# The batch loop of a normalise, project and gate kernel, written out

## What is computed

```
g = group_norm(x, 32 groups, eps=1e-5)            # over 4 channels and all pixels of a batch
u, var = mean and variance of g over the channels, for each pixel (ddof=1)
n = (g - u) / (sqrt(var) + 1e-6)
out = x + g * (einsum('bchw,oc->bohw', n, W) + b)
```

## Time and profile before

| | |
|---|---|
| median of three runs | 2007.43 us (2003.10 to 2016.56) |
| the profiled execution | 2013.78 us |
| its span, first to last instruction | 2012.0 us |
| mean granted TensorE clock | 0.977 |
| VectorE busy | 1774.8 us, 88% |
| TensorE busy | 1762.1 us, 88% |
| GpSimd busy | 1456.2 us, 72% |
| ScalarE busy | 1433.4 us, 71% |
| read / written | 398.80 MB / 268.44 MB, 332 GB/s over the span |

### The profile page before, as it was taken

One profiled execution on the slowest core, in us unless ns is written; L12 is line 12 of the kernel. 1 busy time (PEld: TensorE's weight loads), 2 busy tenths in 40 slices (PEclk: granted clock), 3 DMA queues, 4 the chain that ended last, 5 costly groups with the idle time before them and its releaser, 6 DMA issues.

```text
span 2012.0 us, 61495 instructions
## 1 busy us (share of the span) xinstructions
PE 1762.1 (88%) x22562; PEld 998.3 (50%) x22562; DVE 1774.8 (88%) x2120; ACT 1433.4 (71%) x2498; POOL 1456.2 (72%) x1684
## 2 busy tenths in 40 slices
PE   0089998999789997999979999699998999899997
PEld 0055555555445554555535555355554555455553
DVE  5669989999879997899869998799987999898896
ACT  5598876888568884788838887488875888544441
POOL 0068777888668876688758887588876888688885
PEclk9989999999999998999989999899998999999999
DMA  9989998999879998899978999699997999844665
GB/s 379 372 323 354 375 349 290 412 374 385 326 266 395 372 391 288 310 386 376 379 260 328 385 390 355 240 381 376 382 343 253 409 353 393 315 190 189 263 248 203
DMA packets 184241, 671.78 MB, mean 334 GB/s; under 512 B 20688, under 2 KB 21072, under 8 KB 183888
## 3 DMA queue, kind: packets, MB, share of 16 engines
q1 hardware_dynamic: 110160, 398.85, 53.7%
q10 hardware_dynamic: 73728, 268.47, 33.7%
HBM read 398.80 MB, written 268.44 MB: 332 GB/s over the span
## 4 chain that ended last, share of the span: by engine, by line
PE 48%; DVE 20%; issue 12%; DMA 11%; POOL 3%; ACT 3%; SPq 2%; ACTq 1%; POOLq 0%; DVEq 0%
PE proj_ps L753 27%; PE sums_ps L742 12%; PE factor_ps L728 8%; DMA tiles<-x 7%; DVE scaled L652 7%; DMA out<-tiles 4%; DVE bn L696 4%; DVE tiles L665 3%; DVE bn L697 3%; SPq L428 2%; ACT unused L529 1%; POOL tiles L472 1%; POOL tiles L461 1%; ACT squares L544 1%; DVE gn L600 1%
## 5 line engine op out<-in xcount | busy, mean ns | idle before, releaser
L753 PE MATMUL proj_ps<-scaled,w_t 128*128 128x512 f32 x2048 | 1014.6, 619 | 0.2 <-DVE scaled L652 0.2
L472 POOL TENSOR_SCALAR tiles<-tiles,out_shift 128x1024 f32<-128x1024 f32 x512 | 576.8, 1127 | 242.3 <-DVE tiles L665 232.5
L665 DVE SCALAR_TENSOR_TENSOR tiles<-proj_ps,gate_shift,tiles 128x1024 f32<-128x1024 f32 x512 | 643.8, 1257 | 50.4 <-PE proj_ps L753 48.3
L544 ACT ACTIVATE squares<-tiles 128x1024 f32<-128x1024 f32 x512 | 537.3, 1049 | 195.3 <-POOL tiles L461 77.5
L461 POOL TENSOR_SCALAR tiles<-tiles,norm_scalars 128x1024 f32<-128x1024 f32 x512 | 614.6, 1201 | 81.5 <-DMA tiles<-x 67.6
L652 DVE TENSOR_TENSOR scaled<-tiles,factor_ps 128x1024 f32<-128x1024 f32 x512 | 619.8, 1211 | 58.2 <-PE factor_ps L728 41.3
L529 ACT ACTIVATE unused<-tiles,bn 128x1024 uint8<-128x1024 f32 x560 | 634.8, 1134 | 0.6 <-DVE bn L697 0.6
L753 PEld LDWEIGHTS proj_ps<-scaled,w_t 128*128 128x128 f32 x2048 | 356.8, 195 | 253.2 <-issue 252.2
L728 PE MATMUL factor_ps<-pieces,pick_sb 128*128 128x128 bf16 x4096 | 323.2, 223 | 138.6 <-DVE scaled L652 72.5
L742 PEld LDWEIGHTS sums_ps<-tiles,const_sb 128*32 128x32 f32 x8192 | 196.2, 110 | 404.9 <-issue 274.6
L728 PEld LDWEIGHTS factor_ps<-pieces,pick_sb 128*128 128x128 bf16 x4096 | 234.8, 99 | 250.3 <-issue 128.6
(11 more groups left out here) (56 smaller groups left out, 693.2 us busy)
## 6 DMA issues: line engine op xcount, KB each, us to landing
tiles<-x SPq DMA_DIRECT2D x760, 512.0 KB, 9.4
out<-tiles ACTq DMA_DIRECT2D x512, 512.0 KB, 7.0
const_sb<-const SPq DMA_DIRECT2D x1, 193.5 KB, 2.3
scaled<-w SPq DMA_DIRECT2D x1, 64.0 KB, 2.2
scaled<-ident SPq DMA_DIRECT2D x1, 64.0 KB, 2.0
pick_sb<-pick SPq DMA_DIRECT2D x1, 8.0 KB, 2.1
bias_sb<-bias SPq DMA_DIRECT2D x1, 0.5 KB, 2.1
```

Source lines behind the costliest of these rows:

```text
L472: nc.gpsimd.tensor_scalar(place(s), place(s), 1.0, out_shift[:, 0:1], ALU.mult, ALU.add).then_inc(finished, 1)
L544: nc.scalar.activation(squares[:, step % 2, :], place(step), ACT.Square).then_inc(squared, 1)
L665: nc.vector.scalar_tensor_tensor(out=place(s), in0=proj_ps[:, s % 2, :], scalar=gate_shift[:, 0:1], in1=place(s), op0=ALU.add, op1=ALU.mul ...
L753: mm = nc.tensor.matmul(proj_ps[:, s % 2, h:h + BANK], w_t[:, :], scaled[:, s % 2, h:h + BANK], start=True, stop=True)
```

## The change

The loop is gone. `over_periods` calls `period` for every batch from -1 to 8 with a plain number, so each engine's instructions for batches 1 to 6 stand in the program one after the other. Each wait value and address is a constant. `wait_apart` is replaced by the plain wait everywhere, and the semaphore `wait_passed`, which nobody waited for, is dropped. Which operations are issued, their order on each engine and what each waits for stay.

```diff
-        wait_passed = sem("wait_passed")
...
-        def wait_apart(eng, semaphore, value):
-
-
-            eng.wait_ge(semaphore, value)
-            if not isinstance(value, int):
-                eng.sem_inc(wait_passed, 1)
...
-        def over_periods(eng, period, looks_ahead=False):
-
-
-
-            looped = batches - 1 - looks_ahead
-            ahead = {"more": True} if looks_ahead else {}
-            no_more = {"more": False} if looks_ahead else {}
-            period(-1, own=False, before=False, nxt=True, **(ahead if batches > 1 else no_more))
-            period(0, own=True, before=False, nxt=batches > 1, **(ahead if batches > 2 else no_more))
-            if looped > 1:
-                with eng.Fori(1, looped) as b:
-                    period(b, own=True, before=True, nxt=True, **ahead)
-            for b in range(max(looped, 1), batches):
-                period(b, own=True, before=True, nxt=b < batches - 1, **no_more)
-            period(batches, own=False, before=True, nxt=False, **no_more)
+        def over_periods(period, looks_ahead=False):
+
+            for b in range(-1, batches + 1):
+                ahead = {"more": b + 2 < batches} if looks_ahead else {}
+                period(b, own=0 <= b < batches, before=b > 0, nxt=b + 1 < batches, **ahead)
...
         def at_batch(array, b, s):
-            if isinstance(b, int):
-                return array[b, :, columns(s)]
-            return array[bass.ds(b, 1), :, columns(s)].rearrange("a c n -> (a c) n")
+            return array[b, :, columns(s)]
...
-                wait_apart(pool, gated, b * slots + step - LAG_OUT + 1)
+                pool.wait_ge(gated, b * slots + step - LAG_OUT + 1)
```

More of the change, by code:

```diff
@@ L204, in bn_before @@
     def bn_before(n):
-        return 0 if isinstance(n, int) and n == 0 else n * plan.bn_slots + (first_plan.bn_slots - plan.bn_slots)
+        return 0 if n == 0 else n * plan.bn_slots + (first_plan.bn_slots - plan.bn_slots)
     def act_before(n):
-        if isinstance(n, int) and n == 0:
+        if n == 0:
             return 0
@@ L397, in wait_item_done @@
             def wait_item_done(n, i):
-                of = first_plan if isinstance(n, int) and n == 0 else plan
+                of = first_plan if n == 0 else plan
                 if of.engine[i] == "dve":
-                    wait_apart(sp, bn_done, bn_before(n) + (of.index[i] + 1))
+                    sp.wait_ge(bn_done, bn_before(n) + (of.index[i] + 1))
                 else:
-                    wait_apart(sp, act_done, act_before(n) + 2 * (of.index[i] + 1))
+                    sp.wait_ge(act_done, act_before(n) + 2 * (of.index[i] + 1))
             def wait_buffer_free(tenant, b):
                 for (kind, i), back in places.predecessors(tenant):
-                    if not isinstance(b, int) or 0 <= b - back + (kind == "stats") < batches:
+                    if 0 <= b - back + (kind == "stats") < batches:
                         break
@@ L417, in wait_buffer_free @@
                     n = b - back if kind == "stream" else b - back + 1
-                    wait_apart(sp, stored[p], (n * len(stores[p]) + stores[p].index(s) + 1) * 16)
+                    sp.wait_ge(stored[p], (n * len(stores[p]) + stores[p].index(s) + 1) * 16)
             def load(tenant, b):
@@ L440, in period @@
                         load(tenant, b + 1)
-            over_periods(sp, period, looks_ahead=True)
+            over_periods(period, looks_ahead=True)
             for p in range(BUFFERS):
@@ L450, in norm @@
                 if s == 0:
-                    wait_apart(pool, gn_step, (batch + 1) * GN_STEPS)
+                    pool.wait_ge(gn_step, (batch + 1) * GN_STEPS)
                     if own:
-                        wait_apart(pool, normed, batch * slots)
+                        pool.wait_ge(normed, batch * slots)
                     nc.gpsimd.tensor_copy(norm_scalars[:, :], new_scalars[:, 0:2]).then_inc(norm_scalars_set, 1)
-                    wait_apart(pool, norm_scalars_set, batch + 1)
+                    pool.wait_ge(norm_scalars_set, batch + 1)
                 if s in streamed_slots:
                     turn, uses = places.turn(("stream", s), "stream")
-                    wait_apart(pool, stream_loaded[held_by(s)], (batch * uses + turn + 1) * 16)
+                    pool.wait_ge(stream_loaded[held_by(s)], (batch * uses + turn + 1) * 16)
                 nc.gpsimd.tensor_scalar(place(s), place(s), norm_scalars[:, 0:1], norm_scalars[:, 1:2],
@@ L466, in finish @@
                     if before:
-                        wait_apart(pool, finished, b * slots)
+                        pool.wait_ge(finished, b * slots)
                     nc.gpsimd.tensor_copy(out_shift[:, :], mean).then_inc(out_shift_set, 1)
-                    wait_apart(pool, out_shift_set, b + 1)
-                wait_apart(pool, gated, b * slots + step - LAG_OUT + 1)
+                    pool.wait_ge(out_shift_set, b + 1)
+                pool.wait_ge(gated, b * slots + step - LAG_OUT + 1)
                 nc.gpsimd.tensor_scalar(place(s), place(s), 1.0, out_shift[:, 0:1],
@@ L475, in correct @@
             def correct(done):
-                wait_apart(pool, approx_done, done)
-                wait_apart(pool, miss_done, done)
+                pool.wait_ge(approx_done, done)
+                pool.wait_ge(miss_done, done)
                 nc.gpsimd.tensor_tensor(miss[:, :], miss[:, :], approx[:, :], ALU.mult).then_inc(miss_scaled, 1)
-                wait_apart(pool, miss_scaled, done)
+                pool.wait_ge(miss_scaled, done)
                 nc.gpsimd.tensor_tensor(miss[:, :], miss[:, :], approx[:, :], ALU.mult).then_inc(miss_squared, 1)
             def split_first(done):
-                wait_apart(pool, piece_a_done, done)
+                pool.wait_ge(piece_a_done, done)
                 nc.gpsimd.tensor_tensor(factor[:, :], factor[:, :], piece[:, :], ALU.subtract).then_inc(rest_done, 1)
             def split_second(done, step):
-                wait_apart(pool, piece_b_done, done)
+                pool.wait_ge(piece_b_done, done)
                 nc.gpsimd.tensor_tensor(pieces[:, (step - LAG_FIT) // SPLIT % 2, :], factor[:, :], piece[:, :],
@@ L502, in period @@
                     if root_of is not None:
-                        wait_apart(pool, root_sq_done, root_of)
+                        pool.wait_ge(root_sq_done, root_of)
                         nc.gpsimd.tensor_tensor(miss[:, :], var[:, :], miss[:, :], ALU.subtract).then_inc(miss_done, 1)
@@ L510, in period @@
                         split_second(fit_of, step)
-            over_periods(pool, period)
+            over_periods(period)
         @block.scalar
@@ L525, in statistics @@
                     done = 2 * a + which
-                    if not isinstance(n, int) or n > 0 or done >= 2:
+                    if n > 0 or done >= 2:
                         act.wait_ge(act_done, act_before(n) + (done - 1))
@@ L565, in period @@
                     if (s := behind(step, LAG_STORE, own, before)) is not None:
-                        wait_apart(act, finished, b * slots + step - LAG_STORE + 1)
+                        act.wait_ge(finished, b * slots + step - LAG_STORE + 1)
                         b_of = b if step >= LAG_STORE else b - 1
                         act.dma_start(at_batch(out, b_of, s), place(s)).then_inc(stored[held_by(s)], 16)
-            over_periods(act, period)
+            over_periods(period)
         @block.vector
@@ L598, in gn_scalars @@
                     bn_part = of.bn_slots / slots
-                    wait_apart(dve, bn_done, bn_before(n) + of.bn_slots)
+                    dve.wait_ge(bn_done, bn_before(n) + of.bn_slots)
                     then(nc.vector.bn_aggr(cell(0, 2), bn_of(of)[:, 0:2 * of.bn_slots, :].rearrange("p a b -> p (a b)")))
@@ L631, in gn_scalars @@
                     then(nc.vector.tensor_scalar(cell(11), cell(11), 0.5, None, ALU.mult))
-                    if not isinstance(n, int) or n > 0:
+                    if n > 0:
                         dve.wait_ge(out_shift_set, n)
@@ L703, in period @@
                         gn_scalars(b + 1, 3, of)
-            over_periods(dve, period)
+            over_periods(period)
         @block.tensor
@@ L722, in spread @@
                     pe.wait_ge(pieces_done, b * sets + (step - LAG_SPREAD) // SPLIT + 1)
-                if step != LAG_SPREAD or not isinstance(b, int) or b > 0:
+                if step != LAG_SPREAD or b > 0:
                     pe.wait_ge(scaled_done, b * slots + step - LAG_SPREAD)
@@ L749, in project @@
                 pe.wait_ge(scaled_done, count + 1)
-                if step >= LAG_FACTOR + 2 or not isinstance(b, int) or b > 0:
+                if step >= LAG_FACTOR + 2 or b > 0:
                     pe.wait_ge(gated, count - 1)
@@ L775, in period @@
                         sums(b, step, before)
-            over_periods(pe, period)
+            over_periods(period)
```

## The result

Written out, the kernel takes 1958.01 us (median of 4 runs, 1953.25 to 1963.90) against 2009.5 us before (4 runs, 2003.10 to 2016.56). The ratio is 0.9744, 95% interval 0.9701 to 0.9788. The forecast was 1962 us. The profiled execution took 1956.86 us with a span of 1955.1 us; the one of before had 2012.0.

A forecast was written before the change was run, and what follows sets the result against it. The prediction saw VectorE and TensorE packed at 88%, with removable idle time at the loop's five jumps back. 54.7 us won minus 9.6 lost gave 45.1 us gained, 1962 us, range 1948 to 1986.

The forecast's parts named there:

- What bounds the kernel: Two engines 88% busy, no single large wait; five jumps back at batch borders cost 10.9 us each, 54.7 us.
- The mechanism: After each jump back of the loop, instructions of the target, then those behind it, are not at hand; engines idle.
- The phase: From L468 to the next L455, constants release GpSimd sooner, lengthening VectorE's L675: 1.6 us a batch, 9.6 us lost.
- The sum: Whole kernel: 54.7 us won by removing five jumps minus 9.6 us lost gives 45.1 us gained, 1962 us.
- the main term: Batch borders of the loop: five jumps back removed, 10.9 us each, 54.7 us gained.
- The transfers: Rival: memory cannot keep 364 GB/s batch after batch, only 356.5; 18 us gained are left, 1989 us; chance 0.12.
- Nothing gained: Rival: straight code stalls likewise once a batch, or branches are worth only what they read; 2007 us; chance 0.08.
- slower: Rival: L675's extra 831 ns enters the path in all 16 sets of six batches, 80 us lost, 2032 us; chance 0.04.

The follow-up runs named there:

- the hinted loop: The kernel before, its loop, registers and increments kept, plus a hint at the top of each pass telling the fetcher where the loop's branch goes: 1959.54 us.

## Why the prediction held, step by step

*What bounds the kernel.* Right. The price of a batch border, read from the distance of two marks with and without a jump, was 10.4 us by the marks and 10.9 by whole batches. The runs say 10.4 (three jumps for 31.2 us), 9.8 (five hinted ones for 49.1 us), and 10.0 by the marks after. The lower of the two prices was the better one; 54.7 us was some 5 too much, since batch 1 of that one execution, the base of the difference, was a little short in its undisturbed part too (192.2 us against 192.8 as the mean of batches 1 to 6 in either kernel), which makes 3 of the 5.

*The mechanism*, instructions not at hand after a jump, was argued from the 3.4 to 6.0 us of the taken branch beside 83 ns of the untaken one. It is now shown: with a hint the same branch takes 361 ns and the border costs next to nothing, and each of TensorE's two stalls holds one 16 KB packet of instructions. The 108 ns of the Trainium skill (Advanced Engine Details and Errata, Control Flow Timing) has the order of TensorE's untaken branch (83 ns) and of the other engines' branches (40 to 63 ns), but isn't the price of a jump; another page of it, Runtime: NRT & Kernel Launch, section Instruction fetch mechanics, does say that a taken branch to a target outside the two fetched blocks must wait for a fetch. The trace agrees, and adds the size: 3.4 to 6 us at the branch on TensorE, and 2.7 to 4.6 us once more two matmuls later.

*The phase*, 9.6 us lost: this term of the sum was mis-sized; as a net it is nothing. The plainest evidence is the hinted loop, which keeps registers, increments and the short L675 and ran 1959.5 us against 1958.0 with constants. L675 went to 1072 ns in all batches as said, and a single increment that mostly undoes it is worth 8 to 9 us over all eight batches, so perhaps 6 to 7 over the six that the change touched (an estimate, by the share of batches). What the step left out is the other side of the same change: GpSimd's other operations are released sooner too, named in the prediction and put at nothing, and delaying them again cost about 9 us (1967 against 1958). The prediction's 0.2 us for this is the whole pause between L479 and L481; in the written-out trace 0.08 us of it remains, so the increment's share is 0.10. The stretch from L468 to the next L455, on which the 1.6 us a batch rested, has a mean of 192.8 us over batches 1 to 6 both with registers and with constants; in batch 0 it was 193.8 before and 191.3 after with no instruction changed. A difference of 1.6 us between two single stretches was inside that spread. The forecast term stood on it, and the right value was zero.

*The sum.* 54.7 - 9.6 = 45.1 forecast, 51.5 measured, of which the jumps are about 50. Two errors in opposite directions, 5 us on the jumps and 10 on the phase, left 5; the rest is the spread of batch 0 and the tail. That 1962 us came within 4 us of the result is partly luck; the main term alone would have come within about as much on the other side.

*The rivals.* The transfers did not take the gain back: batches 1 and 2 moved 359 and 361 GB/s, and no batch was over 233.3 us. The 358 GB/s per core of the Trainium skill (Perfetto Trace Analysis, Engine Utilization), which the prediction took as a limit, is passed by up to one per cent in whole batches, and by more in mid-period (379). The same section calls this figure the share of a core when both cores of a pair use the memory, and says that one core alone can pull more; this kernel runs on one core, so the figure was no bound here. *Nothing gained* and *slower* didn't come about; what the single increment won back of L675's delay came to 8 to 9 us over 128 sets, under 0.1 us each, far from the 0.57 at which it would have decided.

## What to carry to other kernels

Where a loop's body is long, compare its first pass with the later ones between two marks: the difference is the price of a jump, and it may sit on one engine only, here TensorE, with the other engines' stalls beside it. The instruction packets in the list of DMA queues tell whether fetches fall into the idle stretches. Announcing the branch buys the same as writing the loop out, at a fraction of the program. Moving an instruction's release by 0.1 us was worth some 8 us here, where two engines meet on it 128 times, so count both what is released sooner and what it then collides with, and don't take a price of 1 us a batch from one pair of batches.

The best kernel of this study is the written-out one with one increment behind the wait for the gated slot, 1949.5 and 1950.8 us, 8 us under the change.

## What had not been expected

That taking away every jump but TensorE's gains nothing: written out everywhere else, the kernel stayed at 2012.5 us. That its taken branches were no shorter, rather longer, when it reached them sooner (median 4839 against 3674 ns; the single ones overlap, 4.3 to 6.0 us against 3.4 to 6.0). And that a small VectorE operation that starts 0.13 us behind a big one of GpSimd is held until that one ends (1.07 us), while one that starts 0.02 us behind it takes its 0.24 us; Advanced Engine Details and Errata, section GPSIMD Details, in the Trainium skill has the two engines share a read and a write interface, with conflicts when VectorE runs in a two-port mode or reads two inputs from SBUF. The trace agrees for the second kind: L687 reads miss and approx, both in SBUF, and took 1070 ns where it met GpSimd's output shift. L675 has one such input, and no run here shows in which mode it runs, so why it is held stays open.
